# A graph kernel on one Trainium2 core: the second layer sums its neighbours' rows before it projects them, and identity products stand in the tail

## What is computed

```python
# layer 0: masked attention
v, q, k = (relu(einsum('bnd,dh->bnh', x, W) + b) for each of v, q, k)
att = softmax(q @ k.T * mask - NEG * (1.0 - mask), axis=2)
x   = layernorm(x + relu((att @ v) @ Wo + bo))
# layer 1: additive attention over neighbours
h = einsum('bnd,ed->bne', x, W_w) + W_b
e, f = h @ a1, h @ a2
u = mask * exp(e[:, :, None] + f[:, None, :] + a_b)
h_prime = (u / sum(u, axis=2)) @ h
x = layernorm(x + h_prime)
```

## Time and profile before

| | us |
|---|---|
| median of 3 runs | 398.2 (397.88 to 398.65) |
| span of the profiled execution | 397.6 |
| PE busy in it | 382.8 (96%) |
| DVE busy | 345.1 (87%) |
| ACT busy | 331.2 (83%) |
| POOL busy | 280.4 (71%) |

### The profile page before, as it was taken

The page is one execution under the profiler, slowest core; times in us unless marked ns, Lnnn a source line. Parts: engine busy times, 40 slices in busy tenths (PEclk is TensorE's granted clock), DMA queues, the critical chain, the costliest instruction groups (busy, mean ns, idle before and its releaser), DMA issues.

```text
span 397.6 us, 8890 instructions
## 1 busy us (share of the span) xinstructions
PE 382.8 (96%) x2769; PEld 356.5 (90%) x2769; DVE 345.1 (87%) x1056; ACT 331.2 (83%) x661; POOL 280.4 (71%) x258
## 2 busy tenths in 40 slices
PE   8899999999999999999999999999999999999990
PEld 7699988999999999999999998999999999999990
DVE  4887898899779998899969998799988999898976
ACT  5678678997789888898879978898888969999962
POOL 1454862597538995689937999289966799486673
PEclk9999999999999999999999999999999999999997
DMA  7917515836568077663596365870766647968011
GB/s 253 342 43 266 164 65 179 310 122 239 179 219 317 13 281 230 237 249 131 182 298 250 149 235 172 284 296 22 265 202 211 277 157 260 397 220 279 17 55 53
DMA packets 38157, 80.72 MB, mean 203 GB/s; under 512 B 2784, under 2 KB 19680, under 8 KB 38112
## 3 DMA queue, kind: packets, MB, share of 16 engines
q1 hardware_dynamic: 37824, 80.03, 57.7%
q10 hardware_dynamic: 288, 0.14, 0.2%
HBM read 75.96 MB, written 4.19 MB: 202 GB/s over the span
## 4 chain that ended last, share of the span: by engine, by line
PE 87%; DVE 6%; issue 3%; DMA 2%; POOL 1%; SPq 0%; POOLq 0%; DVEq 0%
PE m_ps L1775 14%; PE pt_ps L1727 13%; PE s_ps L1651 7%; PE av_ps L1739 7%; PE av_ps L1741 7%; PE av_ps L1740 7%; PE s_ps L1653 7%; PE s_ps L1652 7%; PE m_ps L1658 6%; PE m_ps L1659 3%; PE m_ps L1651 2%; PE m_ps L1653 2%; PE m_ps L1652 2%; PE m_ps L1756 2%; DMA raw<-in_adj_dram 2%
## 5 line engine op out<-in xcount | busy, mean ns | idle before, releaser
L1041 DVE TENSOR_TENSOR prob_tl<-pt_ps,prob_th 128x512 fp32r<-128x512 f32 x128 | 85.5, 681 | 6.2 <-ACT prob_th L672 6.0
L672 ACT ACTIVATE prob_th<-pt_ps 128x512 fp32r<-128x512 f32 x128 | 74.7, 596 | 18.6 <-PE pt_ps L1727 18.5
L1033 DVE CUSTOM_DVE_ANT_0 prob<-s_ps,penalty 128x1024 f32<-128x1024 f32 x64 | 77.9, 1217 | 10.8 <-PE s_ps L1653 6.6
L404 POOL TENSOR_SCALAR penalty<-raw 128x1024 bf16<-128x1024 f32 x64 | 66.6, 1049 | 26.8 <-DMA raw<-in_adj_dram 13.0
L664 ACT ACTIVATE prob<-prob,neg_max 128x1024 f32<-128x1024 f32 x64 | 73.7, 1152 | 1.9 <-DVE neg_max L1033 1.9
L1727 PE MATMUL pt_ps<-rhs,prob 128*128 128x128 f32 x512 | 73.9, 274 | 0.0
L1739 PE MATMUL av_ps<-prob_th,vh 128*128 128x256 f32 x256 | 73.6, 288 | 0.0
L1741 PE MATMUL av_ps<-prob_th,vl 128*128 128x256 f32 x256 | 72.3, 282 | 0.0
L1740 PE MATMUL av_ps<-prob_tl,vh 128*128 128x256 f32 x256 | 72.3, 282 | 0.0
L606 ACT ACTIVATE adj_t<-adjt_in 128x1024 fp32r<-128x1024 f32 x56 | 59.3, 1062 | 11.2 <-PE m_ps L1775 11.2
L1775 PE MATMUL m_ps<-g,adj_t 128*128 128x258 f32 x448 | 63.1, 287 | 0.4
(11 more groups left out here) (161 smaller groups left out, 918.4 us busy)
## 6 DMA issues: line engine op xcount, KB each, us to landing
raw<-in_adj_dram SPq DMA_DIRECT2D x64, 512.0 KB, 5.6
adjt_in<-in_adj_t_dram SPq DMA_DIRECT2D x56, 512.0 KB, 4.0
x_in<-in_x_dram SPq DMA_DIRECT2D x8, 512.0 KB, 7.0
raw<-in_adj_t_dram SPq DMA_DIRECT2D x8, 512.0 KB, 5.7
raw<-in_x_t_dram SPq DMA_DIRECT2D x15, 256.0 KB, 4.4
out_dram<-out_sb SPq DMA_DIRECT2D x14, 256.0 KB, 4.1
out_dram<-out_sb SPq DMA_DIRECT2D x4, 128.0 KB, 1.8
wb<-in_pack_b_dram SPq DMA_DIRECT2D x1, 320.0 KB, 5.2
```

Source lines behind the costliest of these rows:

```text
L672: sc.activation(prob_th[n % 2][:, tiles(k), (i % 2) * P:(i % 2 + 1) * P], pt_ps[k][:, :].rearrange("p (c n) -> p c n", n=P), ACT.Copy).the ...
L1033: v.tensor_tensor_reduce(out=prob[i % 2][:, :], in0=s_ps[:, :, :].rearrange("p a n -> p (a n)"), in1=penalty[:, n % RING, :], scale=-1.0, ...
L1041: v.tensor_tensor(prob_tl[n % 2][at], pt_ps[k][:, :].rearrange("p (c n) -> p c n", n=P), prob_th[n % 2][at].bitcast(F32), ALU.subtract).th ...
```

## The change

Numbers of lines with the changed kernel are its own.

1. **The order of the second layer.** `g` is now exp(f) times the normalised rows x1 themselves, not h. The last of the 128 features is replaced by the weight exp(f) alone: a normalised row sums to zero, so its last feature follows from the others, and the projection's weights are built accordingly (each row less the last row; the bias stands in the last). The sums of the weighted rows come first (`aggregate`), and the projection of the sums behind them (`project_hp`).
2. **The sums come out transposed.** g is the stationary side now and `adj` the moving one, with 512 columns: 4 products for a call, 32 for a batch. What comes out is what the projection wants as its left side. ACT `at_hi` and DVE `at_lo` (1084) split it, and `hp_out` (1090) adds the two halves of the projection.
3. **The transposes of x1, its split, h_out, agg_out, the denominators' own two steps and `add_wb` are gone.**
4. **e and f** come from x1 by DVE: for each tile two dot products of 128 elements with a prepared row (`row_dots`, 1078), 16 in a batch.
5. **A pass later**: the second residual, its statistics and the last normalisation of a batch run in pass p for batch p-3. There are three buffers of x1 for this, two of the exponentials, and half as many for the split attention result. PSUM banks are given out by a table of numbers instead of by turns.
6. **The tail.** The sums of the last batch are 16 products of 256 columns for each pair of tiles, four pairs. The projection of the last four pairs stands behind the last sum; the fourth waits until the residual of the second has read its bank. Residual and denominators read PSUM directly. `hold_clock` is one identity product and is called 14 times: 3, 2 and 2 times between the projections of the batch before, and 7 times ahead of the last projection.
7. **The orders** of all engines are rewritten. In the head DVE splits the first x before the weights, and the load of the second batch's x is issued before that of the late weights.

```diff
-            def transpose_x1(b, k):
-                pe.wait_ge(x1_done, T * b + (k + 1) * TH)
-                xt = shared("x1t", b, k)
-                for c in range(TH):
-                    last = pe.transpose(blk(xt, c), x1[:, k * TH + c, :], ident)
-                last.then_inc(x1t_full, 1)
...
+            def aggregate(b, j):
+                n = T * b + j
+                k, u = j // TH, j % TH
...
-                    last = pe.matmul(a[:, 0:2 * G1], adj_tile(b, i)[:, c, :],
-                                     g[:, c, :, :].rearrange("p a e -> p (a e)"), start=(c == 0), stop=(c == T - 1))
+                for c in range(2):
+                    pe.matmul(a[:, :], g[:, 2 * u + c, 0, :], adj_tile(b, j)[:, c, :], start=(u == 0 and c == 0), stop=False)
+                    last = pe.matmul(a[:, :], g[:, 2 * u + c, 1, :], adj_tile(b, j)[:, c, :], start=False, stop=(u == TH - 1 and c == 1))
...
+            def row_dots(b, t):
+
+                wait(dve, dots_done, T * b + t - 1)
+                stand_alone(dve)
+                for a in range(2):
+                    last = v.tensor_tensor_reduce(out=spent[:, t % 2, a, :], in0=x1[b % KEPT][:, t, :], in1=dot_row[:, a, :], scale=1.0, scalar=0.0,
+                                                  op0=ALU.mult, op1=ALU.add, accum_out=dots[:, t, a:a + 1])
+                last.then_inc(dots_done, 1)
...
+            def project_hp_pair(r):
+                pe.wait_ge(atl_last, r + 1)
+                hh = shared("hp_last", LAST, r)
...
             def hold_clock():
 
-                pe.wait_ge(ptl_done, 2 * T * B - 1)
-                for _ in range(HOLD):
-                    pe.matmul(pt_ps[0][:, 0:P], ident, ident, start=True, stop=True)
+                pe.matmul(av_ps[:, PAIR:PAIR + P], ident, ident, start=True, stop=True)
```

1469 lines of the change are left out of this document (710 added, 759 removed), and 13 rows, old and new, of tables (HEAD_SLOTS, PASS_SLOTS).

## The result

The changed kernel is **slower**: median 412.95 us (410.63 to 417.55 in four runs) against 398.04 for the kernel before, a ratio of 1.035 with an interval of 1.031 to 1.039. The forecast was 394.0 and its range ended at 399.0. Executions in a slower state of the chip are left out of every ratio, though not of the medians: the 417.55 here, the 405.74 of e8_yield_both and two of e14_half_sums6.

A forecast was written before the change was run, and what follows sets the result against it. TensorE was taken to bound the passes and the tail up to the last matmul. 397.6 - 6.0 (passes) - 1.3 (pass 1) - 0.5 (head) - 0.9 (tail) + 3.5 + 1.0 (collisions) + 0.6 = 394.0 us, range 388.5 to 399.

The forecast's parts named there:

- The price of PE's work in a pass: Each pass: transposes 0.88 us less, sums over neighbours 0.32 less, together 1.20 less; five passes give 6.0.
- The price of a dot product: VectorE in a pass: 16 new dot products at 0.22 us each, 3.5 us, hidden if nothing else holds them.
- Which operations collide: A VectorE instruction with two SBUF inputs stands until GpSimd's running instruction ends: 0.5 us on average, up to 1.1.
- The stretch behind the last sum: End of the kernel: new steps and queueing lengthen 9.50 us to 11.9, bounds 11 and 13.5.
- The identity products: Tail: fourteen at 0.23 us, 3.2 in all; seven before the last sum charged 1.8 with their stops, seven behind free.
- Pass 1: First pass: 2.72 us less PE work, partly lost to growing waits; 1.3 less taken, bounds 0 and 2.7.
- The head: Start of the kernel: earlier first subtraction and scores, 0.5 us less; bounds 1.5 less and 1 more.
- the size of the collisions: Dots ahead of a row maximum stop PE 0.7 us per pass, 3.5 over five; pass 1 and tail 1.0 together.
- DVE's room of 2.6: Each pass: VectorE at 42.8 us against PE's 45.4 leaves 2.6 us, within which the later dots' waits stay hidden.
- rival C: Passes: VectorE becomes the bound, eight of sixteen dots waiting 0.75 us each; 406.5 us, deciding from 3.8 per pass; chance 0.14.
- Before the last sum: ... Sum: ... = -3.3: Tail ahead of the last sum: PE work removed, moved and added, including transposes, sums, projections and identity products, gives 3.3 us less.
- Outside the span: Around the profiled execution: 0.6 us between its 397.6 span and the 398.2 median, added at the end.

The follow-up runs named there:

- e8_yield_both: Changed kernel with GpSimd waiting for dot products in the passes and for dots and g's low parts in the tail: 399.54 us, ratio 1.004.
- e14_half_sums6: Changed kernel without dot products, tail residual on GpSimd held for g's low parts, 16 of batch 6's sum products cut to 2 columns: 399.05 us, ratio 1.001.
- e2_one_input: Changed kernel with each dot product replaced by a plain sum of the same x1 row, one SBUF input instead of two: 398.79 us, ratio 1.001.
- e3_no_dots: Changed kernel with the dot products left out, VectorE writing zeros instead: 399.46 us, ratio 1.002.
- e6_yield_pass: Changed kernel with two more GpSimd waits per pass, mask conversions starting only after the dot products of the moment: 400.68 us, ratio 1.006.
- e12_yield_pass2: Changed kernel with the same two GpSimd waits per pass for dot products, run again on another chip: 403.23 us, ratio 1.014.
- e4_no_holds: Changed kernel without the fourteen identity products of the tail: 413.03 us, ratio 1.036.
- e13_own_g2: Kernel of e11_own_g with splits of the last sums ahead of and between batch 6's statistics, second pair's sums two projections later: 402.56 us, ratio 1.009.
- e11_own_g: Changed kernel with the passes' GpSimd waits, a separate last-batch g buffer, two pairs' sums among batch 6's projections and queues reordered: 406.74 us, ratio 1.020.

## Why the prediction was wrong

**Right steps.**
- The price of PE's work in a pass. The 32 sums come to 7.67 us from start to start, where 64 came to 8.03 by the same count: 0.36 less, forecast 0.32. The transposes are 0.79 less, forecast 0.88. Without collisions a pass takes 45.3 us, forecast 45.4, and PE is busy for all of it (e2_one_input, e3_no_dots, e6_yield_pass).
- The price of a dot product: 0.21 from start to start, forecast 0.22. DVE is busy for 42.1 us in a pass where no dot collides (e12_yield_pass2), under the 42.8 that I had worked out. Without collisions it is hidden, as forecast.
- Which operations collide. The reason named ahead of the result, that an instruction of DVE with two SBUF inputs stands until POOL's running instruction is over, is what e2_one_input and e6_yield_pass show, the second with the operation itself unchanged. The Trainium skill, page "SBUF — State Buffer", section "Who interferes with whom", states it so, and says that on this chip a `tensor_reduce` never contends. Both agree here: 1.11 beside 0.28 for the product, 247 to 282 ns for all 128 reductions.
- The stretch behind the last sum: 12.9 us, and 12.3 in e3_no_dots, forecast 11.9 (11 to 13.5).
- The identity products: charged at 1.8 with the stops that they fill. The runs give nothing for the products (e4_no_holds).
- Pass 1 gained more, 2.4 in place of 1.3, and inside its bounds. The head is 0.8 longer than forecast in the first profile, and within its bounds by luck: in seven of the 14 profiles with the new order it is 2.2 us or more over the 45.14 of before, where my bound was 1.

**Wrong step 1, the size of the collisions.** I took 0.7 us per pass. The passes are 1.0 to 4.2 us over 45.3, 10.5 in all in place of 3.5. I had let only two dot products meet POOL ahead of a row maximum, and had hidden the rest in "DVE's room of 2.6". Three to five of sixteen wait in each of the passes 2 to 6, fewer than rival C's eight. Nor did PE stop at the row maximum, as I had it, but at other things of DVE's queue. The room is an average over the pass, and DVE's idle time does not stand where the waits are. Rival C was to decide from 3.8 us of waits per pass; four of the five measured passes are over the old 46.64 with 3.0 to 4.6 us of lateness, dots and small operations together. Of it 1.0 to 4.2 became time (in the longest pass the granted clock was 0.97 as well, and PE busy for 47.0). So C had the collisions right, with a count and a threshold too high, but not its bound: DVE is idle for 2.1 to 5.3 us of these passes and most dots are short, so it is single delays at places where something waits that cost, and not DVE's work as a whole. The price of all collisions of the dots, for which the sum had 3.5 + 1.0, is measured three ways: 13.1 us (e2_one_input) and 12.4 (e3_no_dots), both against the changed kernel on the same chip, and 11.4 or 8.2 (the two yields, on two chips).

**Wrong step 2, "Before the last sum: ... Sum: ... = -3.3".** Measured: +6.2, and +4.0 in e3_no_dots, which has no dot products. The sum counted PE's work, since PE had been busy for 68.93 of 69.26 us. That was true of the old tail, in which the sums of batch 6 (ending at 370.33) filled PE beside the attention of batch 7. In the changed one they end at 379.72, behind the attention (373.85). Then come the projection of batch 6, its reductions, scales, residual and statistics, and the g of batch 7, in a row over DVE, ACT and POOL, one behind the other in the same queues. Of the +6.2, +7.3 is idle time of PE (7.65 of 75.41 us against 0.33), for which the sum had 0.2, and -1.2 is work (67.76 us), for which it had -3.5: the transposes had taken 1.46 from start to start and not 1.76, the sums cost 0.2 less and not 0.7, and part of the products ran further apart than before. e14_half_sums6 shows that 2.2 us less of PE's work there give no less time. Of the forecast's items the transposes and the old identity products did go, but a term of work taken from an engine is worth little where that engine has stopped setting the time. The step that failed is that I did not follow, ahead of the last sum, the chain that I did follow behind it.

Part of this is a collision too: the second SBUF input of the tail's g (2.8 us of PE's stop in e3_no_dots). But taking it away gave 0.5 us: the last sum came 2.8 us earlier behind the attention, and the stretch behind that sum grew by 2.3. e13_own_g2 shows one link of the chain, the residual of the last batch behind the normalisation of batch 6 in one buffer, and e11_own_g another, `atl` behind the statistics. **What stays open** is how the remaining 6 us divide between the order in the queues of DVE and POOL, the one buffer of the sums (`gs`), and the banks of the last projection: none of the versions that I tried brought the tail below 85 us, and a chain shortened at one place stopped at the next.

**Outside the span** I added 0.6 and it was 1.7: I had set a span of one execution against a median of others. That is 1.1 of the 16.6 us between forecast and the profiled run; the median lies 2.3 us higher still.

**No variant is faster than the kernel before.** The change saves 6.7 us in five passes and 2.5 in pass 1 where no dot collides; the tail takes back 6.3 or more in every variant, and the head 0.3 to 4.3.

## What to carry to other kernels

Before moving work to VectorE, list for each new or changed instruction how many of its inputs are in SBUF, and lay them against GpSimd's timeline at that place; a free engine on average is not a free place in its queue, and two waits that make GpSimd yield gave back 8 to 11 us here. Where a pipeline drains, cost the tail as a chain from the last product of the last batch to its store, over all engines: an engine at 99% in the old order may have nothing to do with the new one's length. And when a computation moves one pass later, ask which batch's work now stands between the last attention and the last sum.
